# Moving a per-channel scale from the transposed activations into the stored weights of an 8-chunk layer

## What is computed

```
def rms(v): return v / (sqrt(mean(v*v)) + 1e-8)             # over a half of 512
h  = layernorm(x)                                           # (4096, 1024) per core
xn = concat(ls_scale * rms(h[:, :512]), rs_scale * rms(h[:, 512:])) * split_scale
K  = sigmoid(xn @ Wk)                                       # 1024 -> 2048
u, g_in, g_out = split(xn @ Wugg, 3)                        # 1024 -> 3 x 2048
h_t = K_{t-1} * h_{t-1} + u_t * sigmoid(g_in_t) * (1 - K_t) # scan over the rows
x  = x + (h * sigmoid(g_out)) @ Wout + layernorm(x)
y  = x + top2_of_4_experts(layernorm(x))                    # gelu(z @ W1 + b1) @ W2 + b2, weighted
```

## Time and profile before

| | |
|---|---|
| times of four runs | 6171.60, 6419.89, 6469.64, 6481.37 us; median 6444.76 |
| the profiled execution, its own time | 6166.49 us |
| its span on the slowest core (core 6) | 6164.9 us |
| spans of the eight cores | 6118.1 to 6164.9 us |
| TensorE matmuls busy | 5021.3 us, 81% of the span |
| ScalarE, VectorE busy | 1532.6 us (25%), 1271.1 us (21%) |
| L813, L765 matmuls | 1839.1 and 1823.7 us |
| L507, L611 matmuls | 722.0 + 219.8 and 244.2 us |
| L420 copies | 256 of 367 ns, 94.1 us |
| mean granted TensorE clock of a core | 0.913 to 0.918 |

### The profile page before, as it was taken

One profiled execution on the slowest core, in us unless ns is written; L12 is line 12 of the kernel. 1 busy time (PEld: TensorE's weight loads), 2 busy tenths in 40 slices (PEclk: granted clock), 3 DMA queues, 4 the chain that ended last, 5 costly groups with the idle time before them and its releaser, 6 DMA issues.

```text
span 6164.9 us, 63948 instructions; the slowest of 8 cores (6118.1 to 6164.9 us)
## 1 busy us (share of the span) xinstructions
PE 5021.3 (81%) x22689; PEld 2232.7 (36%) x23137; DVE 1271.1 (21%) x3340; ACT 1532.6 (25%) x2596; POOL 330.4 (5%) x495
## 2 busy tenths in 40 slices
PE   3657777878887888978898788887888788897998
PEld 1223333333333333333343334333333333333443
DVE  3230000421015200241104310043011520024000
ACT  2121221222322233122322222222232223312212
POOL 2100000000000000000000000000000000000000
PEclk9778889989998999989999799998999899998999
DMA  8969999323332344414344144432333233441443
GB/s 131 170 125 201 193 198 237 110 103 130 130 138 101 131 133 132 170 63 144 116 137 178 42 145 134 147 134 95 131 128 141 107 116 130 131 169 63 136 146 121
DMA packets 306913, 830.56 MB, mean 135 GB/s; under 512 B 82724, under 2 KB 115620, under 8 KB 257448
## 3 DMA queue, kind: packets, MB, share of 16 engines
q0 software_dynamic: 186528, 429.95, 27.8%
q1 hardware_dynamic: 94152, 308.41, 14.9%
q10 hardware_dynamic: 25920, 88.09, 4.3%
HBM read 809.61 MB, written 104.86 MB: 148 GB/s over the span
## 4 chain that ended last, share of the span: by engine, by line
PE 66%; DMA 14%; DVE 8%; ACT 6%; issue 4%; DVEq 1%; POOL 0%; ACTq 0%; SPq 0%; POOLq 0%
PE pb L813 26%; PE pb L765 24%; PE pb L507 12%; DMA slab<-W 6%; PE pb L611 3%; DMA sW<-slab 3%; DMA slab<-Wugg 2%; ACT xnf L420 1%; ACT tmpev L827 1%; ACT tmpev L831 1%; DMA h_sb<-sWA 1%; DMA sWA<-slab 1%; DMA slab<-sW 1%; DVE stv L629 1%; DVEq L87 1%
## 5 line engine op out<-in xcount | busy, mean ns | idle before, releaser
L813 PE MATMUL pb<-slab,h_sb 128*128 128x512 bf16 x8025 | 1839.1, 390 | 264.5 <-ACT xnf L420 125.3
L765 PE MATMUL pb<-xnf2h,slab 128*128 128x512 bf16 x8023 | 1823.7, 387 | 206.0 <-DMA slab<-W 86.3
L813 PEld LDWEIGHTS pb<-slab,h_sb 128*128 128x128 bf16 x8192 | 815.3, 100 | 1285.0 <-issue 373.5
L765 PEld LDWEIGHTS pb<-xnf2h,slab 128*128 128x128 bf16 x8192 | 809.3, 99 | 1217.8 <-issue 302.3
L774 ACT ACTIVATE h_sb<-pb,b1s 128x512 bf16<-128x512 f32 x1024 | 703.9, 687 | 1121.8 <-PE pb L765 1109.1
L507 PE MATMUL pb<-xnf,slab 128*128 128x512 bf16 x3134 | 722.0, 388 | 59.4 <-DMA slab<-Wugg 33.7
L836 DVE TENSOR_TENSOR acc<-acc,tmpev 128x1024 f32<-128x1024 f32 x128 | 156.8, 1225 | 2424.7 <-ACT tmpev L831 2424.5
L827 ACT ACTIVATE tmpev<-pb,wsb 128x512 f32<-128x512 f32 x128 | 88.0, 687 | 1822.2 <-PE pb L813 1801.0
L507 PEld LDWEIGHTS pb<-xnf,slab 128*128 128x128 bf16 x3200 | 313.0, 100 | 467.4 <-issue 125.2
L259 POOL DMA_DIRECT2D slab<-sW x224 | 144.8, 647 | 3841.6 <-PE pb L765 1812.7
L507 PE MATMUL pb<-xnf,h_sb 128*128 128x512 bf16 x875 | 219.8, 412 | 93.7 <-DMA h_sb<-sWA 59.9
(11 more groups left out here) (129 smaller groups left out, 1906.5 us busy)
## 6 DMA issues: line engine op xcount, KB each, us to landing
slab<-sW SPq DMA_DIRECT2D x224, 1024.0 KB, 5.4
slab<-sW POOLq DMA_DIRECT2D x224, 1024.0 KB, 5.8
slab<-W POOLq DMA_DIRECT2D x64, 1024.0 KB, 24.8
sW<-slab ACTq DMA_DIRECT2D x64, 1024.0 KB, 12.2
slab<-sWA SPq DMA_DIRECT2D x42, 1024.0 KB, 7.5
slab<-sWA POOLq DMA_DIRECT2D x42, 1024.0 KB, 7.8
x_sb<-x_in POOLq DMA_DIRECT2D x32, 512.0 KB, 6.2
sWA<-slab ACTq DMA_DIRECT2D x16, 1024.0 KB, 11.6
```

The lines of the kernel that those rows point to most:

```text
L765: e.matmul(pb[bk][:, 0:512], lhsT=slab[:, sl, (kc * 4 + jp) * 128:(kc * 4 + jp) * 128 + 128], rhs=xnf2h[:, kc, :], start=(kc == 0), stop=( ...
L813: e.matmul(pb[m * 2 + h][:, 0:512], lhsT=h1_sb[:, j, m * 128:(m + 1) * 128], rhs=slab[:, sl, jj * 1024 + h * 512:jj * 1024 + h * 512 + 512 ...
```

## The change

- In `load_piece_cast_wa` the store of the slab to `sWA`, until now issued as soon as the load had landed, is taken out.
- In the attention loop of chunk 0, after the 32 matmuls of a j, VectorE multiplies the slab in place, eight blocks of 128x512 bf16, each by its channel block's column of `sc_sb`; the first of these waits for the matmuls. Then the store to `sWA` is issued from ScalarE, ahead of the three sigmoids, and waits for the last multiplication. `store_free` and `region_done` take its token. So `sWA` holds scaled weights.
- `emit_ln1_tr` gets the argument `scaled`. With it (chunk 0 alone, whose matmuls use the unscaled slab) the eight scaled copies stay. Without it (chunks 1 to 7) ScalarE makes one plain copy per bank, 128x512.

```
                             inc=f"dZ{s}")
-            tokS = p.op("scalar",
-                        lambda e, s=s, j=j: e.dma_start(
-                            out=sWA[j].rearrange("p k w c -> p (k w c)"),
-                            in_=slab[:, s, :]),
-                        waits=[tokL], inc=f"dT{s}")
-            store_free[s] = tokS
-            region_done.setdefault("WA", [None] * 4)[s] = tokS
+            region_done.setdefault("WA", [None] * 4)
...
-        def emit_ln1_tr(mt, tap):
+        def emit_ln1_tr(mt, tap, scaled=False):
...
-                for q in range(4):
-                    kc = half * 4 + q
+                if scaled:
+                    for q in range(4):
+                        kc = half * 4 + q
+                        ev = p.op("scalar",
+                                  lambda e, kc=kc, q=q, mt=mt, bk=bk:
+                                  e.activation(xnf[:, kc, mt * 128:(mt + 1) * 128],
+                                               pbb[bk][:, q * 128:(q + 1) * 128],
+                                               AF.Copy, scale=sc_sb[:, kc:kc + 1]),
+                                  waits=[tk, tSc] if q == 0 else [], inc="Sc")
+                else:
                     ev = p.op("scalar",
-                              lambda e, kc=kc, q=q, mt=mt, bk=bk:
-                              e.activation(xnf[:, kc, mt * 128:(mt + 1) * 128],
-                                           pbb[bk][:, q * 128:(q + 1) * 128],
-                                           AF.Copy, scale=sc_sb[:, kc:kc + 1]),
-                              waits=[tk, tSc] if q == 0 else [], inc="Sc")
+                              lambda e, half=half, mt=mt, bk=bk:
+                              e.copy(xnf[:, half * 4:half * 4 + 4, mt * 128:(mt + 1) * 128],
+                                     pbb[bk][:, 0:512].rearrange("p (q c) -> p q c", q=4)),
+                              waits=[tk], inc="Sc")
...
-                    xnf_ready = emit_ln1_tr(mt, emit_ln1_tile(ch, mt))
+                    xnf_ready = emit_ln1_tr(mt, emit_ln1_tile(ch, mt), scaled=(ch == 0))
...
                 if sl is not None:
                     free_slot(sl, tmm)
+                if ch == 0:
+                    tsc_ = None
+                    for kc in range(KC):
+                        tsc_ = p.op("vector",
+                                    lambda e, sl=sl, kc=kc:
+                                    e.tensor_scalar_mul(slab[:, sl, kc * 512:(kc + 1) * 512],
+                                                        slab[:, sl, kc * 512:(kc + 1) * 512],
+                                                        sc_sb[:, kc:kc + 1]),
+                                    waits=[tmm, tSc] if kc == 0 else [], inc="V")
+                    tokS = p.op("scalar",
+                                lambda e, sl=sl, j=j: e.dma_start(
+                                    out=sWA[j].rearrange("p k w c -> p (k w c)"),
+                                    in_=slab[:, sl, :]),
+                                waits=[tsc_], inc=f"dT{sl}")
+                    store_free[sl] = tokS
+                    region_done["WA"][sl] = tokS
```

## The result

The changed kernel's median over nine runs is 6145.08 us; beside it the kernel before has 6429.91 us over thirteen. The ratio after / before is **0.9934, 95% interval 0.9909 to 0.996**, about 41 us less (25 to 56). A second series with the same kernel gave 0.9924 (0.9886 to 0.9963), 47 us less (23 to 70). The forecast was 63 us less: the sign came out, but a quarter to a third of the forecast gain is missing. The first series excludes the forecast, the second alone would not.

What follows compares the result with a forecast made beforehand. Full DMA was taken to bound chunk 0 and TensorE chunk 1, the slowest core setting the time. Gain 70 plus 3 in chunk 0 minus price 10 gave 63 us less than 6166.5, say 6104; range 6060 to 6420.

Steps and rivals of the forecast that it cites:

- The gain: Layer norm woven into experts 1 to 3, chunks 1 to 6: 9.3 us a chunk from copies, 2.4 from clock, 70 together.
- One turn of that chain: Chunk 0's attention: matmuls, scaling, store issue, sigmoids and scan take 21 us for two slabs, which have 26 us.
- I take nothing: Beginning of chunk 0's attention: the load of j = 4 goes out about 9 us later, but no cost is counted.
- still every 13 us: Sign of being right: slabs of chunk 0's attention keep coming every 13 us.
- The queue still does not run empty: Middle of chunk 0's attention: with fewer loads queued they land sooner, so the cast-load queue stays filled; no cost.
- The end: End of chunk 0's attention: the last Wout load goes out 8 to 14 us later; bounds 0 to 17, taken 10.
- Chunk 0's share in the gain: Chunk 0's experts: full DMA mostly hides the faster copies; bounds 0 to 11.7 us, taken 3.
- own range: Whole kernel: 6085 at best, 6127 at worst, 15 us added either way for the cores' spread, so 6070 to 6142.
- Latency, not queueing: Chunk 0's attention: loads take 38.4 us however few stand before them; 8 us slower, 6174; chance 0.08, far end 0.03.
- VectorE holds up the loads' issue: Chunk 0's attention: scalings stop POOL's loads, twelve slabs 5.2 us later each, 62 us; 6166, no change; chance 0.06.
- The clock still falls at expert 3: Expert 3, chunks 1 to 6: the clock gain is missing, 49 us less in all, 6117; chance 0.15.
- The gain is hidden: Experts 1 to 3: something else holds L813, so only 3 - 10 is left, 6174; chance 0.03.

Runs made afterwards that it cites:

- late store: Changed kernel without the eight multiplications, store still after the slab's matmuls, factor left out in chunks 1 to 7: one time for the comparison, 6171.15 us.
- store from SyncE: Changed kernel with the store issued by SyncE instead of ScalarE: 6084.52 and 6130.56 us; timed again, 0.9906 against the kernel before.
- out of place: Changed kernel, but VectorE writes the scaled copy into idle h1_sb as a slab lands and SyncE stores that: 0.9904 against the kernel before.
- price alone: Changed kernel with scaling and late store kept, but scaled copies back in all chunks: 1.0026 against the kernel before, 16 us more.
- the three kernels without the ring: Changed kernel with late store (6171.15 us), store from SyncE (0.9906) or scaling out of place (0.9904), ratios against the kernel before.
- the last experiment: Changed kernel with each plain copy of a chunk's last tile made three times: standstill 4.57 us, six chunks 4367.5 us, 5.5 more a chunk.
- the first experiment: Changed kernel with plain copies in chunks 1 to 7 only, store back where it was, no scaling: 0.9891 against the kernel before, 67 us less.

## Why the prediction was half right

**The gain: right.** 9.3 us a chunk from the shorter string and 2.4 from the clock were forecast, 70 for six chunks; the mean over the cores is 68.7. The standstills came out as 7.63, 8.36 and 1.88 (forecast 7.4, 8.6, 1.9). The other kernels repeat it: these chunks take 4335.6 to 4339.7 us with plain copies (late store, store from SyncE, out of place) and 4406.8 with scaled ones (price alone).

**The failed step** is the pair "One turn of that chain is 8.6 (matmuls) + 5.2 + 0.4 + 2.1 + 4.4 = 21 us for two slabs ... has 26 us and is covered" and, of the beginning, "I take nothing". The chain was followed through `attn_ev_v`, which spans two j, and its other closure was overlooked: the scan of j stands in VectorE's list ahead of the scaling of j + 1, so scaling, store issue, sigmoids and scan close upon themselves every slab. The prediction's own terms give 5.2 + 0.4 + 2.1 + 4.4 = 12.1 us for it, with the scaling's measured 3.6 it is 10.5, and the trace shows 10.95.

The second half of the error was the comparison with 13.1 us a slab. That is core 6's pace once the loads set it (12.1 is the mean of six cores); the first slabs lie in their slots already and passed at 7.6 us. There the ring is the slowest thing, and j = 4 starts 12 us later (130.5, mean of the five executions with this loop, against 118.4 of the two with the old one). In the steady part the slabs come 12 us apart in both ((261.6 - 130.5) / 11 = 11.9 after, (251.0 - 118.4) / 11 = 12.1 before). That the forecast's "still every 13 us" came out so nearly is luck: before, the loads set this pace, now the ring does, and the two happen to be equally long. So the lost time isn't made good: j = 15 is 10.6 us late. "The queue still does not run empty" failed with it: the loads wait for slots that turn later, and the queue's share falls from 102 or 103.5 to 92 to 95. It is back at 99.6 to 103.5 in the three kernels without the ring. None of the forecast's rivals held this path.

**The end: right in size, in part by luck.** Taken were 10 us, bounds 0 to 17, for the late load of Wout alone. Measured are two pieces: the tail grows from 6.9 to 12.4 us (scaling and store issue stand between the last matmuls and the last scan, which the forecast did not name), and from Wout to W1 it takes 94.4 instead of 89.0, 5.4 more, together 10.9. So half of the size came from a piece that the forecast did not have. The second piece stays, 94.9 to 98.0, in the kernels that issue the store late without the ring, so it goes with the late store; that it is the late Wout load alone is argued from the restart at 305.44, not shown. Out of place, where no slot waits for a store, it is 92.7 in one execution, hardly below the lowest of the changed loops (92.9).

**Chunk 0's share in the gain: nothing seen.** 3 us were taken. From W1 to the end of chunk 0 the kernels with plain copies take 666 us at the mean (nine executions of the table), those with scaled ones 667 (two). Single executions lie 13 us apart, so 3 us could not have been seen.

**The sum again**, by what was measured: 69 - 10.6 - 10.9 + 0 = 47 us less, against 63 forecast and 41 (25 to 56) and 47 (23 to 70) timed. The missing term is the one put at zero. Its size rests on five executions against two, and those two are 8.6 us apart at W1. The time of 6145.08 lies in the stated range of 6060 to 6420, and 3 us above the own range of 6070 to 6142.

**The rivals.** *Latency, not queueing* fell. The queue of the casting loads and their landings (L292), 120 to 200 us, core 0 of the changed kernel:

```profile
q0 software_dynamic: 26079, 6.58, 93.7%
...
DMA to landing us min/median/max: 7.7/12.6/22.3
```

Before they took 26.7 us at the median of the whole loop, 27.6 in this stretch; now they land in half of that. Four loads come every 12 us, so by these times some 9 were under way at once before and some 4 are now, an estimate. The queue's share alone does not tell it: with the store from SyncE it is back at 103.5, and they land in 14.9 us at the median (core 3). *VectorE holds up the loads' issue* fell: no issue became longer. The two do meet, with the roles turned (last section). *The clock still falls at expert 3* fell for the 1.88 us of this change; behind the 4.57 us of the last experiment the clock did fall. *The gain is hidden* fell with the first experiment.

## What to carry to other kernels

When an instruction is put into a loop, follow not only its semaphores but the lists that it joins: two engines that each hold two steps of the loop in order close a ring, and the ring's length is the loop's pace, whatever a wait two turns back allows. Compare that length with the pace of every part of the loop, the first turns included, where preloaded data let it run faster than the steady state. A DMA's issue that has to wait belongs in a queue with nothing urgent behind it: moving one such issue from ScalarE to SyncE gave back 11 us at Wout (282.4, the mean of five executions, to 271.0), though the total time did not part from the changed kernel's beyond the intervals.

## What had not been expected

The scaling, all 128 on core 0 (min/median/max ns, first and last start):

```profile
L523 DVE TENSOR_SCALAR slab<-slab,sc_sb x128: 352/353/807, 95.6 to 276.4; 128x512 bf16<-128x512 bf16 x128
```

0.353 us lies between the bounds of 0.15 and 0.55. The Trainium skill, "VectorE: DVE Perf Modes", section on the TRN2 errata, gives the formula from which 0.19 us was estimated. The same section of the Trainium skill says that the formula comes out too short, with a fixed part of about 150 cycles instead of 58 measured on a copy; an estimate with that is (150 + 128) / 0.96 GHz = 290 ns. The trace has 0.353 us for an instruction with nothing beside it, so here the measurement decides.

The long ones belong to instructions beside the issue of a casting load: in the second series, all cores, none of the 795 without such an issue takes over 0.355 us, and 160 of the 229 with one take over 0.4. Core 6 of the changed kernel in the first series, VectorE and then POOL:

```profile
94.66 3.58 DVE L523 TENSOR_SCALAR slab<-slab,sc_sb 128x512 bf16<-128x512 bf16 x8 [12.01 <-PE pb L508]
...
129.38 5.18 DVE L523 TENSOR_SCALAR slab<-slab,sc_sb 128x512 bf16<-128x512 bf16 x8
```

```profile
130.01 0.88 POOL L286 DMA_DIRECT2D slab<-Wk  x1 [10.31 <-DMA sWA<-slab]
130.88 2.64 POOL L292 DMA_DIRECT2D slab<-Wugg  x3
```

Eight in a row take 3.58 us alone and 5.18 us when POOL issues four loads at the same time. The issues become no longer: L286 takes 0.878 to 1.002 us beside a scaling and 0.873 to 1.006 us in the kernel before, which has none. The Trainium skill, "SBUF — State Buffer", section "Who interferes with whom", says that a VectorE instruction in a two-port mode and a GpSimd instruction exclude each other, and that whichever issues first keeps the other out. The trace agrees that they disturb each other; here it is VectorE that pays, 1.6 us for this slab, and the ring's turn is longer by it. That it is these ports, and in which mode the scaling ran, no run here shows.
